# Scores issued sooner and in pairs, transposes behind the units with fixed keys: a two-layer recurrent and attention block on one core

## The chip, the cores and the metric

The kernel runs on one core of one Trainium2 chip. The time is the device time in microseconds of one execution; three runs of the kernel before gave 791.44 to 791.93 us, with a median of 791.5. Most executions of a kernel agree within 0.3%.

## What is computed

The input has 16 sequences of 256 tokens with 256 features. Layer 0 normalises, runs a complex diagonal recurrence with 32 states beside a feed-forward part of 1024 units with GELU, and adds the product of the two. Layer 1, where the change is, does for each sequence:

```
q  = xn @ Wq                       # 16 heads, 128 plain + 64 rotary columns
kv = xn @ Wkv_a                    # 64 latent + 64 rotary columns
c  = rmsnorm(kv[:64]);  k_rope = rope(kv[64:])
scores = causal(q . k) / sqrt(192);  attn = softmax(scores)
s  = (attn @ v) @ Wo
z  = xn @ base_w + base_b + 2 * sum_e gate_e * (xn @ A_e) @ B_e   # top 2 of 8 experts
x  = x + s * silu(z)
```

The weights of keys and values are folded into those of queries and output beforehand, so the scores are taken against the latent (64) and rotary (64) columns, and the weighted sum is one over latents.

## The kernel before

**Steps.** Layer 1 runs in steps n = 10b + m: sequence b, m from 0 to 9. Each engine has its own program (one function for each block), with the same loop over n, and semaphores between them. Every engine runs its instructions in the order written. In step n TensorE issues, in this order (L889 to L923): LoRA's projection `lo` of the next sequence (m = 8); the weighted sum `pv` of the sequence before, in four banks v0 to v3 (m = 5); query blocks `q0` to `q7` of the next sequence (m = 2: q1, q2; 3: q3, q0; 6: q5; 7: q7; 9: q6, q4); unit n of the scores; `tk`, the transposes of the next sequence's keys (m = 8); `ty`, four transposes of the normalised rows of the sequence after next (m = 6); `mi`, the small projections that give latents, rotary keys, LoRA's inner part and the router (m = 8 and 9); `tm`, two transposes of LoRA's gated inner part (m = 6); and `o0`, `o1`, the output blocks of the sequence before (m = 6 and 7). Query, output, LoRA and small projections are made of three FP32R products each (L549).

**Units.** A sequence has ten units of scores: four W (two tiles of 224 and 256 columns' worth of keys, queries as weights), four M (three tiles of 128, 160 and 192), both at L773, and two T, "with fixed keys" (L766), where the keys are the weights, 32 columns of the array for each head, and which are issued together at m = 5. Unit n goes to one of two banks, n modulo 2, and waits for the maximum of unit n - 2 (`mx`, L1610). Then VectorE masks and takes the maximum (L1608), ScalarE the exponential (L1065), VectorE the reciprocal (L1615), GpSimd the product (`normalise`, L2051), VectorE the turn (L1631, L1644), each for its own unit in the order of n. The sums of the weighted sum are split by ScalarE (oh, L1078) and VectorE (ol, L1653) into a high and a low part, pair 0 and pair 1 of banks for the first half of the queries (qt = 0), then for the second (EVAC, L51).

**The ring.** All jobs of TensorE but the scores take turns in six banks of PSUM, in the order of `shared_bank_order` (L142), which is the order of issue. `free_shared` (L659) makes job k wait until job k - 6 has been read. For v0, `freed_by` (L340) asks for `oth` and `otl` up to pair 0 of both halves, the third of four.

**VectorE's step** (L1809 to L1857): subtractions of the latents (m = 5), `y_low` (m = 7), `gated_out`, the turning of queries (L1579), the gate's thread, reciprocal, turn of weights, `weigh` (L1561), `gate_sum` (L1556, m = 8, needs `lo`), and last the maximum of unit n.

**GpSimd's step** (L2146 to L2168): the key's turn (L2022, m = 1), which waits for the two small projections as ScalarE copied them, the factors of the norms (L2083 to L2103, m = 1 and 2), the gate's product (L2038, m = 5), sums of queries (L2044, L2045), residual (L2113), `normalise(n - 2)`.

Of the kernel before, what the change touches and what calls it, by code (L numbers as in the profile page):

```python
# [15 lines left out]
NB = 16  # L16
# [22 lines left out]
UNITS = 10  # L39
# [7 lines left out]
TOTAL = NB * UNITS  # L47
# [8 lines left out]
Q0_AT = {}  # L56
LAST_LORA, LAST_SUM, LAST_SPREAD = 152, 153, 149
KV_AT, GATE_AT, SCALE_AT, NORM_AT, YN_AT = 1, 2, 6, 0, 4
TURN_AT, TM_AT, TK_AT, LORA_AT, MISC_AT = 6, 6, 8, 8, (8, 9)
GATE_REST = 9  # L60
PRODUCT_AT = 5

TURN_FIRST = (5, 13, 20, 28, 36, 44, 52)
BU_AT = (7, 14, 20, 28, 36, 44, 52, 60)
# [72 lines left out]
def with_next(n):  # L137

    return UNITS <= n < TOTAL - 1 and unit(n)[1] == unit(n + 1)[1] == "T"


def shared_bank_order():  # L142

    js = [
        ("q", 1), ("q", 3), ("ty", 1), ("q", 0), ("q", 5), ("q", 7), ("q", 2), ("q", 4), ("lo", 0), ("mi", 2), ("mi", 3), ("q", 6),
    ]
    for n in range(STEPS):
        b, m = n // UNITS, n % UNITS
        if (d := lora_of(n)) is not None:
            js.append(("lo", d))  # L150
        if (d := due("V", n, 0)) is not None:

            if len(js) % 2:
                js.append(("pad", len(js)))
            js += [("v", 4 * d + i) for i in range(4)]
        js += [("q", u) for u in Q0_AT.get(n, ())]
        if b + 1 < NB:
            js += [("q", 8 * (b + 1) + u) for u in queries_at(b + 1, m)]
        if m == TK_AT and b + 1 < NB:
            js.append(("tk", b + 1))  # L160
        if m == TURN_AT and b + 2 < NB:
            js.append(("ty", b + 2))
        if m in MISC_AT and b + 2 < NB:
            js.append(("mi", 2 * (b + 2) + MISC_AT.index(m)))
        if m == TM_AT and b + 1 < NB:
            js.append(("tm", b + 1))
        for qt in range(2):
            if (d := due("O", n, qt)) is not None:
                js.append(("o", 2 * d + qt))
    return js  # L170
# [27 lines left out]
def build(nc, x, consts, rows, vecs, w1t, w2t, b1c, bt, ct, nuth, wqn, wkbt, wqr, wkva, wvbt, wo,  # L198
          baset, lorab, loraa, routert, out):
    ctx = ExitStack()  # L200
    with ctx:
# [134 lines left out]
        def jof(kind, i):  # L336
            return bank[ring[jplace[(kind, i)] % RING]]
# [206 lines left out]
        def _(e):  # L544
# [232 lines left out]
            def l1_pv(b, blocks, units):  # L777

                first, end = blocks
                C = C4[b % 2]  # L780
                w.wait_ge("pt", UNITS * b + units)
                w.wait_ge(f"c{b % 2}", 256 * (b // 2 + 1))
                for i in range(4):
                    free_shared("v", 4 * b + i)
                if blocks == LAST_BLOCKS:

                    w.wait_ge("otl", 4 * b + 2)
                for kb in range(end):
                    q = max(first, kb)
                    at = slice(64 * (kb % 2), 64 * (kb % 2) + 64)  # L790
                    for i in range(4):
                        rows_ = slice(32 * i, 32 * i + 32)
                        sums = jof("v", 4 * b + i).rearrange("p (u t) -> p u t", u=2)
                        for half in range(2):
                            j = e.matmul(sums[64 * half:64 * half + 64, :, 32 * q:32 * end],  # L795
                                         C[rows_, kb // 2, at], PT[rows_, 2 * half:2 * half + 2, kb, q:end, :],
                                         start=(kb == 0), stop=(kb == end - 1), skip_group_check=True)
                j.then_inc(SEM["pv"], 1)
# [19 lines left out]
            for g in range(L0_STEPS):  # L818
# [40 lines left out]
                c, r = divmod(g - 6, 8)  # L859
                if r == 0 and 0 <= c < NC - 1:  # L860
                    l0_turn(c + 1, 1)
                if g in TURN_FIRST and g != 13:
                    c = TURN_FIRST.index(g)
# [25 lines left out]
            for n in range(STEPS):  # L889
                b, m = n // UNITS, n % UNITS  # L890
                if (d := lora_of(n)) is not None:
                    l1_lora(d)
                for qt in range(2):
                    if (d := due("V", n, qt)) is not None and (qt or d == NB - 1):
                        if d < NB - 1:
                            l1_pv(d, ALL_BLOCKS, UNITS)
                        else:
                            l1_pv(d, LAST_BLOCKS if qt else FIRST_BLOCKS, UNITS if qt else FIRST_DONE)
                for u in Q0_AT.get(n, ()):
                    l1_q(0, u)  # L900
                if b + 1 < NB:
                    for u in queries_at(b + 1, m):
                        l1_q(b + 1, u)
                if n < TOTAL and not (n and with_next(n - 1)):
                    l1_s(n)
                    if with_next(n):
                        l1_s(n + 1)
                if m == TK_AT and b + 1 < NB:
                    free_shared("tk", b + 1)
                    l1_tk(b + 1, jof("tk", b + 1))  # L910
                if m == TURN_AT and b + 2 < NB:
                    free_shared("ty", b + 2)
                    l1_turn(b + 2, jof("ty", b + 2))
                if m in MISC_AT and b + 2 < NB:
                    i = 2 * (b + 2) + MISC_AT.index(m)
                    free_shared("mi", i)
                    l1_misc(b + 2, i % 2, jof("mi", i))
                if m == TM_AT and b + 1 < NB:
                    free_shared("tm", b + 1)
                    l1_tm(b + 1, jof("tm", b + 1))  # L920
                for qt in range(2):
                    if (d := due("O", n, qt)) is not None:
                        l1_out(2 * d + qt)  # L923

        @block.scalar
        def _(e):
# [258 lines left out]
            for n in range(STEPS):  # L1185
                b, m = n // UNITS, n % UNITS
                if n == 5:
                    place(e, w, 1, 0, (2, 3))
                c, i = b, m
                if 0 <= c < NB - 1 and i == TM_AT:  # L1190
                    mids(c + 1, jof("tm", c + 1))
                c, i = b, m
                if 0 <= c < NB - 2 and i == TURN_AT:
                    y_high(c + 2, jof("ty", c + 2))
                c, i = divmod(n - 1, UNITS)
                if 0 <= c < NB - 1 and i == TK_AT:
                    keys(c + 1, jof("tk", c + 1))
                for u in Q0_AT.get(n - 1, ()):
                    if u % 2 == 0:
                        queries(0, u)  # L1200
                if n == TOTAL - UNITS:
                    exps(n - 1)
                c, i = divmod(n - 1, UNITS)
                if 0 <= c < NB - 1:
                    for u in queries_at(c + 1, i):
                        if u % 2 == 0:
                            queries(c + 1, u)
                if n and (d := sum_of(n - 1)) is not None:
                    gate_tanh(d)
                if m == YN_AT and b + 2 < NB:  # L1210
                    normed(b + 2)
                for qt in range(2):
                    if (d := due("L", n, qt)) is not None:
                        latents(d, qt)
                if m == SCALE_AT and b + 1 < NB:
                    weighed(b + 1)
                c, i = divmod(n - 1, UNITS)
                if 0 <= c < NB - 2 and i in MISC_AT:
                    t = MISC_AT.index(i)
                    misc(c + 2, t, jof("mi", 2 * (c + 2) + t))  # L1220
                if 0 <= n - 1 < TOTAL and n != TOTAL - UNITS:
                    exps(n - 1)
                c, i = divmod(n - 1, UNITS)
                if 0 <= c < NB - 1 and i == GATE_AT:
                    gate_exp(c + 1)
# [634 lines left out]
        def _(e):  # L1860
# [287 lines left out]
            for n in range(STEPS):  # L2148
                b, m = n // UNITS, n % UNITS
                if m == KV_AT and b + 1 < NB:  # L2150
                    key_turn(b + 1)
                    chain = factors(b + 2)
                go(chain, 3)
                if m == PRODUCT_AT and b + 1 < NB:
                    gate_product(b + 1)
                for u in Q0_AT.get(n - 1, ()):
                    if u % 2 == 1:
                        queries_sum(0, u // 2)
                c, i = divmod(n - 1, UNITS)
                if 0 <= c < NB - 1:  # L2160
                    for u in queries_at(c + 1, i):
                        if u % 2:
                            queries_sum(c + 1, u // 2)
                for qt in range(2):
                    if (d := due("C", n, qt)) is not None:
                        residual(2 * d + qt)
                if 0 <= n - 2 < TOTAL:
                    normalise(n - 2)  # L2168


def shape_constants():
# [86 lines left out]
```

## Time and profile before

| what | value |
|---|---|
| median of 3 runs | 791.5 us |
| profiled execution, its own time | 791.67 us |
| its span, first to last instruction | 789.9 us |
| busy of the span: TensorE, its weight load | 778.6 us, 711.5 us |
| VectorE, ScalarE, GpSimd | 681.7, 524.5, 479.5 us |
| TensorE's granted clock | 0.999 of full speed |
| chain that ended last, share of TensorE | 92% |

The profiled execution lies 1.77 us above its span and 0.17 us above the median. Layer 0 fills the first 260 us or so, layer 1 the rest; steps of layer 1 repeat sequence by sequence. A busy TensorE is one whose matmuls follow each other without a gap, whatever each of them costs.

### The profile page before, as it was taken

How to read it: one execution, taken by the hardware profiler on the slowest of the kernel's cores; microseconds unless marked ns; L12 is line 12 of the kernel's file. 1: busy time of each engine (PE TensorE's matmuls, PEld its weight loads, DVE VectorE, ACT ScalarE, POOL GpSimd, SP SyncE). 2: the span in 40 equal slices, each digit the busy share in tenths (PEclk: the TensorE clock that was granted, in tenths of full speed). 3: DMA queues.
4: the chain of work that ended last, by engine and by line, in shares of the span. 5: the costliest groups of instructions: out<-in, count | busy, mean ns of one | idle time of the engine just before them, and what ended most of it. 6: DMA issues, size and time to landing. Idle time of an engine off the chain costs nothing.

```text
span 789.9 us, 23152 instructions
## 1 busy us (share of the span) xinstructions
PE 778.6 (99%) x7976; PEld 711.5 (90%) x7976; DVE 681.7 (86%) x2616; ACT 524.5 (66%) x1612; POOL 479.5 (61%) x1278
## 2 busy tenths in 40 slices
PE   9999999999999999999999999999999999999988
PEld 7889889888889889898998989899898998989867
DVE  6998897888688899989898998989989898998885
ACT  5554454445555787777767777677777867777682
POOL 6880202202236696776867768686776867768673
PEclk9999999999999999999999999999999999999999
DMA  8600220000002222322222322223222222322220
GB/s 302 253 2 2 62 82 27 1 1 1 1 15 52 40 46 52 61 54 36 48 46 50 64 39 50 40 46 55 56 55 35 48 46 49 63 39 53 34 52 28
DMA packets 101334, 41.15 MB, mean 52 GB/s; under 512 B 91744, under 2 KB 98400, under 8 KB 100576
## 3 DMA queue, kind: packets, MB, share of 16 engines
q1 hardware_dynamic: 98896, 38.89, 22.1%
q8 instruction: 63, 1.03, 0.5%
q10 hardware_dynamic: 2320, 0.79, 0.4%
q14 instruction: 55, 0.45, 0.2%
HBM read 14.47 MB, written 4.19 MB: 24 GB/s over the span
## 4 chain that ended last, share of the span: by engine, by line
PE 92%; DVE 4%; ACT 1%; POOL 1%; issue 1%; ACTq 0%; POOLq 0%; DVEq 0%
PE bank L549 63%; PE bank L773 11%; PE bank L795 8%; PE bank L766 3%; PE bank L629 2%; PE bank L815 1%; PE bank L566 1%; DVE SM L1608 1%; PE bank L681 1%; ACT SM L1065 1%; DVE PT L1631 1%; PE bank L641 1%; PE bank L655 1%; POOL SM L2051 1%; PE bank L700 0%
## 5 line engine op out<-in xcount | busy, mean ns | idle before, releaser
L1065 ACT ACTIVATE SM<-SM,stb 128x224 f32<-128x224 f32 (+7 forms) x512 | 207.2, 407 | 62.7 <-DVE stb L1608 58.2
L2051 POOL TENSOR_SCALAR SM<-SM,stb 128x224 f32<-128x224 f32 (+7 forms) x512 | 195.2, 396 | 67.5 <-DVE stb L1615 66.1
L549 PE MATMUL bank<-yh,wq_lo 128*128 128x256 f32 x512 | 150.6, 294 | 0.0
L549 PE MATMUL bank<-yh,wq_hi 128*128 128x256 f32 x512 | 144.7, 283 | 0.0
L549 PE MATMUL bank<-yl,wq_hi 128*128 128x256 f32 x512 | 144.6, 282 | 0.0
L773 PE MATMUL bank<-KT,QT 128*128 128x192 f32 (+4 forms) x640 | 120.9, 327 | 1.7 <-DVE stb L1608 1.7
L1608 DVE CUSTOM_DVE_ANT_0 SM<-bank,CONST 128x224 f32<-128x224 f32 (+3 forms) x320 | 97.2, 348 | 23.3 <-PE bank L773 20.9
L1631 DVE STREAM_TRANSPOSE PT<-SM 128x128 f32<-128x128 f32 (+2 forms) x232 | 99.7, 462 | 16.7 <-PE bank L795 16.7
L773 PEld LDWEIGHTS bank<-KT,QT 128*128 128x128 f32 x640 | 97.5, 190 | 5.3 <-DVE stb L1608 3.6
L549 PEld LDWEIGHTS bank<-yh,wq_lo 128*128 128x128 f32 x512 | 97.1, 190 | 1.4
L549 PEld LDWEIGHTS bank<-yh,wq_hi 128*128 128x128 f32 x512 | 97.1, 190 | 0.0
L549 PEld LDWEIGHTS bank<-yl,wq_hi 128*128 128x128 f32 x512 | 97.0, 189 | 0.0
L1065 ACT ACTIVATION_READ_ACCUMULATOR SM<-SM,stb 128x1 f32 x512 | 96.9, 189 | 0.0
L950 ACT ACTIVATE hs<-bank,B 128x512 f32<-128x512 f32 x64 | 44.0, 688 | 75.3 <-PE bank L549 70.2
L2044 POOL TENSOR_TENSOR QA<-QA 128x256 f32<-128x256 f32 x62 | 45.9, 740 | 58.7 <-DVE QA L1579 58.7
L1037 ACT ACTIVATE QT<-bank 64x512 f32<-64x512 f32 x128 | 75.6, 590 | 6.5 <-PE bank L549 5.0
L1579 DVE TENSOR_TENSOR QA<-bank,TR 128x512 f32<-128x512 f32 x124 | 79.4, 683 | 0.1
L549 PE MATMUL bank<-woe_hi,ol 128*128 128x256 f32 x256 | 75.4, 294 | 0.7 <-issue 0.7
L549 PE MATMUL bank<-w2h,hl 128*128 128x256 f32 x256 | 74.0, 289 | 0.2 <-DVE w2l L1352 0.2
L549 PE MATMUL bank<-w2h,hh 128*128 128x256 f32 x256 | 72.4, 283 | 0.0
L549 PE MATMUL bank<-w2l,hh 128*128 128x256 f32 x256 | 72.3, 283 | 0.0
L549 PE MATMUL bank<-woe_hi,oh 128*128 128x256 f32 x256 | 72.1, 281 | 0.0
(229 smaller groups left out, 2068.9 us busy)
## 6 DMA issues: line engine op xcount, KB each, us to landing
QT<-QA SPq DMA_DIRECT2D x240, 64.0 KB, 2.1
PT<-KV SPq DMA_DIRECT2D x256, 16.0 KB, 1.8
out<-fo SPq DMA_DIRECT2D x32, 128.0 KB, 2.0
X<-in_x SPq DMA_DIRECT2D x7, 512.0 KB, 11.5
stage<-in_wqn SPq DMA_DIRECT2D x2, 1024.0 KB, 5.3
stage<-in_wo SPq DMA_DIRECT2D x2, 1024.0 KB, 4.9
stage<-in_w1t SPq DMA_DIRECT2D x4, 256.0 KB, 5.0
stage<-in_w2t SPq DMA_DIRECT2D x2, 512.0 KB, 6.2
```

Of the source, the lines that this page charges most:

```text
L549: i = e.matmul(dst, a, b, start=(first and j == 0), stop=(last and j == 2), skip_group_check=skip)
L766: j = e.matmul(sbank[n % 2][32 * i:32 * i + 32, at:to], KT[b % 3][:, p, 32 * kb:32 * kb + 32], Q[:, :, kb:3, i, :], start=True, stop=True)
L773: j = e.matmul(sbank[n % 2][:, at], Q[:, q, :, :].rearrange("p h c -> p (h c)"), KT[b % 3][:, p, 0:32 * q + 32], start=True, stop=True)
L795: j = e.matmul(sums[64 * half:64 * half + 64, :, 32 * q:32 * end], C[rows_, kb // 2, at], PT[rows_, 2 * half:2 * half + 2, kb, q:end, :], ...
L950: e.activation(hs[g % 2][:, :], fbank[g % 2][:, :], ACT.Gelu, bias=B1[:, g % 8:g % 8 + 1]).then_inc(SEM["gelu"], 1)
L1037: i = e.activation(QT[r, (2 * b + g // 2) % 3, p, :, g % 2:4:2, :].rearrange("p n j c -> p j n c"), src[r, :, :, :], ACT.Copy)
L1065: i = e.activation(M[:, at], M[:, at], ACT.Exp, bias=S[:, 0, j:j + 1], scale=-1.0, accum_out=S[:, 1, j:j + 1])
L1579: i = e.tensor_tensor(A[:, part, :, :, g % 2, :], src, TR[:, part, :].rearrange("p (n c) -> p n c", n=8).unsqueeze(1).broadcast_to([128, 2 ...
L1608: i = e.tensor_tensor_reduce(M[:, at], bk[:, at], mask[:, 224 - 32 * q:256], 1.0, 3e38, ALU.add, ALU.min, S[:, 0, j:j + 1])
L1631: return e.transpose(PT[:, slot, 0:k, q:q + some, :].rearrange("p k q c -> p q k c"), src)
L2044: e.tensor_tensor(A[:, 0, 0, :, :], A[:, 0, 0, :, :], A[:, 1, 1, :, :], ALU.subtract)
L2051: i = e.tensor_scalar(P[:, at], P[:, at], S[:, 2, j:j + 1], 1.0, ALU.mult, ALU.mult)
```

## The change

Constants, the helper that says which units a step issues, the order of the ring and the two loops change. The order of the ring and TensorE's program are the same list, written twice.

- Units: for b = 2 to 14 nothing is issued at m = 0, 1 and 2 (b = 14: units 0 and 1 of the last sequence sooner); the step m = 7 issues units 7 and 8, m = 8 unit 9 and the next sequence's unit 0, m = 9 the next one's units 1 and 2.
- `ty` and `tm` go ahead of the step's query block (from b = 1), so they come directly behind the T units of m = 5. At b = 0 `tm` stays last.
- `tk` goes from m = 8 to m = 7 (from b = 1), behind the scores; `mi` goes ahead of the scores (from b = 1).
- GpSimd: `PRODUCT_AT` from 5 to 4, and the call goes from ahead of the sums of queries to behind `normalise`.

```diff
-TURN_AT, TM_AT, TK_AT, LORA_AT, MISC_AT = 6, 6, 8, 8, (8, 9)
+TURN_AT, TM_AT, TK_AT, TK_FIRST, LORA_AT, MISC_AT = 6, 6, 7, 8, 8, (8, 9)
-PRODUCT_AT = 5
+PRODUCT_AT = 4
+def scores_at(n):
+    if not 0 <= n < TOTAL:
+        return ()
+    b, m = divmod(n, UNITS)
+    if b and m < 3 and b > 1 and (b < NB - 1 or m < 2):
+        return ()
+    if b and b < NB - 1 and m > 6:
+        return {7: (n, n + 1), 8: (n + 1, n + 2), 9: (n + 2, n + 3) if b < NB - 2 else (n + 2,)}[m]
+    if n and with_next(n - 1):
+        return ()
+    return (n, n + 1) if with_next(n) else (n,)
+def tk_of(n):
+    b, m = divmod(n, UNITS)
+    return b + 1 if m == (TK_AT if b else TK_FIRST) and b + 1 < NB else None
...
+                if m == TURN_AT and b + 2 < NB:
+                    free_shared("ty", b + 2)
+                    l1_turn(b + 2, jof("ty", b + 2))
+                if m == TM_AT and b and b + 1 < NB:
+                    free_shared("tm", b + 1)
+                    l1_tm(b + 1, jof("tm", b + 1))
                 for u in Q0_AT.get(n, ()):
                     l1_q(0, u)
                 if b + 1 < NB:
                     for u in queries_at(b + 1, m):
                         l1_q(b + 1, u)
-                if n < TOTAL and not (n and with_next(n - 1)):
-                    l1_s(n)
-                    if with_next(n):
-                        l1_s(n + 1)
...
-                if m in MISC_AT and b + 2 < NB:
+                if m in MISC_AT and 0 < b and b + 2 < NB:
                     i = 2 * (b + 2) + MISC_AT.index(m)
                     free_shared("mi", i)
                     l1_misc(b + 2, i % 2, jof("mi", i))
...
+                for i in scores_at(n):
+                    l1_s(i)
+                if tk_of(n):
+                    free_shared("tk", tk_of(n))
+                    l1_tk(tk_of(n), jof("tk", tk_of(n)))
...
-                if m == PRODUCT_AT and b + 1 < NB:
-                    gate_product(b + 1)
...
                 if 0 <= n - 2 < TOTAL:
                     normalise(n - 2)
+                if m == PRODUCT_AT and b + 1 < NB:
+                    gate_product(b + 1)
```

The order of the ring (`shared_bank_order`) changes in the same way.

## Rows read from the trace of the kernel before

**Rows 1.** TensorE's waits, 290 to 750 us: us in total, times, longest

```profile
PE bank L795 <- DVE PT L1631: 0.4, 1, 0.4
```

**Rows 2.** Busy time by engine in one step, from one weighted sum to the next

```profile
core 0: us, PE busy (x) PEld busy (x) DVE busy (x) ACT busy (x) POOL busy (x), PEclk, DMA share, GB/s
494.14:528.08 33.94, 33.94 (x400) 31.75 (x399) 30.49 (x141) 25.26 (x89) 24.93 (x66) 1.00 0.26 49
```

**Rows 3.** Timeline of TensorE behind that weighted sum: start, busy us, line, what, count

```profile
498.29 1.52 PE L766 MATMUL bank<-QT,KT 128*32 128x192 f32 x48
499.74 0.38 PE L549 MATMUL bank<-yh,wq_lo 128*128 128x256 f32 x1
499.96 0.28 PE L549 MATMUL bank<-yl,wq_hi 128*128 128x256 f32 x1
...
501.27 0.60 PE L681 MATMUL bank<-CONST,yn 128*128 128x128 f32 x4
501.71 0.38 PE L706 MATMUL bank<-CONST,ML 128*128 128x128 f32 x2
501.84 0.37 PE L549 MATMUL bank<-woe_hi,ol 128*128 128x256 f32 x1
502.05 0.28 PE L549 MATMUL bank<-woe_lo,oh 128*128 128x256 f32 x1
```

**Rows 4.** Timeline of VectorE in the same stretch; the last row is the third subtraction alone

```profile
498.41 0.71 DVE L1631 STREAM_TRANSPOSE PT<-SM 128x512 f32<-128x512 f32 x1 [1.20 <-PE bank L795]
499.04 2.71 DVE L1653 TENSOR_TENSOR ol<-bank,oh 128x512 fp32r<-128x512 f32 x4
...
500.46 0.69 DVE L1653 TENSOR_TENSOR ol<-bank,oh 128x512 fp32r<-128x512 f32 x1
```

**Rows 5.** Timeline of TensorE at b = 0, transposes directly behind a fixed-key unit

```profile
266.38 0.66 PE L681 MATMUL bank<-CONST,yn 128*128 128x128 f32 x4
```

**Rows 6.** Timelines around a unit that waited for a maximum, b = 1

```profile
280.79 0.08 DVE L1608 DVE_READ_ACCUMULATOR2_ANT stb<- 128x1 f32 x1
...
280.92 0.19 PEld L773 LDWEIGHTS bank<-KT,QT 128*128 128x128 f32 x1 [0.78 <-DVE stb L1608]
...
280.93 0.49 PE L773 MATMUL bank<-KT,QT 128*128 128x128 f32 x2 [0.38 <-DVE stb L1608]
```

**Rows 7.** Timeline of TensorE: units 8, 0 and 1, 2, 7

```profile
478.08 0.97 PE L773 MATMUL bank<-KT,QT 128*128 128x224 f32 x4
478.89 0.38 PE L700 MATMUL bank<-CONST,KV 128*128 128x128 f32 x2
...
484.22 1.79 PE L773 MATMUL bank<-KT,QT 128*128 128x224 f32 x10
...
485.97 0.28 PE L549 MATMUL bank<-yl,wq_hi 128*128 128x256 f32 x1
...
488.73 0.98 PE L773 MATMUL bank<-KT,QT 128*128 128x128 f32 x6
...
489.67 0.28 PE L549 MATMUL bank<-yl,wq_hi 128*128 128x256 f32 x1
...
506.21 0.98 PE L773 MATMUL bank<-KT,QT 128*128 128x128 f32 x6
```

**Rows 8.** Timeline of VectorE: the gate's sum, unit 8's maximum; unit 6's maximum

```profile
478.28 0.69 DVE L1556 TENSOR_TENSOR PT<-bank,VEC 128x512 f32<-128x512 f32 x1
479.09 0.39 DVE L1608 CUSTOM_DVE_ANT_0 SM<-bank,CONST 128x224 f32<-128x224 f32 x1
...
479.75 0.08 DVE L1608 DVE_READ_ACCUMULATOR2_ANT stb<- 128x1 f32 x1
...
506.67 0.08 DVE L1608 DVE_READ_ACCUMULATOR2_ANT stb<- 128x1 f32 x1
```

**Rows 9.** Timeline of GpSimd: the key's turn and the gate's product

```profile
485.50 0.45 POOL L2022 TENSOR_TENSOR kr<-ML,rope_c 128x128 f32<-128x128 f32 x1
...
499.27 0.61 POOL L2038 TENSOR_TENSOR ML<-ML,lg 128x256 f32<-128x256 f32 x1
```

**Rows 10.** Timeline of VectorE at b = 14, maximum of unit 9

```profile
751.75 0.39 DVE L1608 CUSTOM_DVE_ANT_0 SM<-bank,CONST 128x224 f32<-128x224 f32 x1 [0.70 <-PE bank L773]
```

More of the change, by code:

```diff
@@ L155, in shared_bank_order @@
             js += [("v", 4 * d + i) for i in range(4)]
+        if m == TURN_AT and b + 2 < NB:
+            js.append(("ty", b + 2))
+        if m == TM_AT and b and b + 1 < NB:
+            js.append(("tm", b + 1))
         js += [("q", u) for u in Q0_AT.get(n, ())]
@@ L158, in shared_bank_order @@
             js += [("q", 8 * (b + 1) + u) for u in queries_at(b + 1, m)]
[L159 to L162, printed above, removed]
+        if tk_of(n):
+            js.append(("tk", tk_of(n)))
         if m in MISC_AT and b + 2 < NB:
             js.append(("mi", 2 * (b + 2) + MISC_AT.index(m)))
-        if m == TM_AT and b + 1 < NB:
-            js.append(("tm", b + 1))
+        if n == TM_AT:
+            js.append(("tm", 1))
         for qt in range(2):
@@ L898, in _ @@
                             l1_pv(d, LAST_BLOCKS if qt else FIRST_BLOCKS, UNITS if qt else FIRST_DONE)
+                if m == TURN_AT and b + 2 < NB:
+                    free_shared("ty", b + 2)
+                    l1_turn(b + 2, jof("ty", b + 2))
+                if m == TM_AT and b and b + 1 < NB:
+                    free_shared("tm", b + 1)
+                    l1_tm(b + 1, jof("tm", b + 1))
                 for u in Q0_AT.get(n, ()):
@@ L903, in _ @@
                         l1_q(b + 1, u)
-                if n < TOTAL and not (n and with_next(n - 1)):
-                    l1_s(n)
-                    if with_next(n):
-                        l1_s(n + 1)
[L908 to L913, printed above, removed]
-                if m in MISC_AT and b + 2 < NB:
+                if m in MISC_AT and 0 < b and b + 2 < NB:
                     i = 2 * (b + 2) + MISC_AT.index(m)
@@ L917, in _ @@
                     l1_misc(b + 2, i % 2, jof("mi", i))
-                if m == TM_AT and b + 1 < NB:
-                    free_shared("tm", b + 1)
-                    l1_tm(b + 1, jof("tm", b + 1))
+                for i in scores_at(n):
+                    l1_s(i)
+                if tk_of(n):
+                    free_shared("tk", tk_of(n))
+                    l1_tk(tk_of(n), jof("tk", tk_of(n)))
+                if n in MISC_AT:
+                    i = 4 + MISC_AT.index(m)
+                    free_shared("mi", i)
+                    l1_misc(2, i % 2, jof("mi", i))
+                if n == TM_AT:
+                    free_shared("tm", 1)
+                    l1_tm(1, jof("tm", 1))
                 for qt in range(2):
@@ L1194, in _ @@
                     y_high(c + 2, jof("ty", c + 2))
-                c, i = divmod(n - 1, UNITS)
-                if 0 <= c < NB - 1 and i == TK_AT:
-                    keys(c + 1, jof("tk", c + 1))
+                if n and tk_of(n - 1):
+                    keys(tk_of(n - 1), jof("tk", tk_of(n - 1)))
                 for u in Q0_AT.get(n - 1, ()):
```

## The prediction

> **What bounds the kernel now.** I read the waits of TensorE first, then its own rows over one step of the second layer, then the engines that feed it. Between 290 and 750 us, thirteen and a half steps of one sequence each, TensorE waited once, 0.4 us [rows 1]. From one weighted sum (L795) to the next it takes 33.94 us and is busy for 33.94 [rows 2]; the clock is at the upper level (2.4 GHz) throughout. The stream itself is the bound there: a reordering can gain only what the stream loses where one kind of matmul follows another, and any wait that it makes is paid in full. VectorE is busy for 30.49 of the 33.94 us, so it can't catch up much. Last I read the order in which PSUM banks go round: job k of the shared list waits for job k-6.
>
> **The change, part by part**, for the steps n = 10b + m with b = 1 to 13, which are 13 steps alike.
>
> *The ring of six banks.* Both orders have 20 jobs a step, 4 of them the weighted sums v0 to v3. Behind them came q5, ty, tm, o0, q7, o1; so tm took over v0's bank. Now it is ty, tm, q5, o0, q7, tk: ty and tm take banks of q3 and q0, long read, and q5 takes v0's. freed_by gives v0's bank free after the third of the four subtractions of L1653, since pair 0 is read for both halves of the queries. VectorE waits 1.20 us for the end of the weighted sum, turns one unit's weights (0.71) and subtracts from 499.04 on; the third ends at 500.46 + 0.69 = 501.15 [rows 4]. Before, tm started at 501.71, behind it. Now to q5: the fixed-key units run 498.29 to 499.74, the four transposes ty take 0.44 and 0.06 for the exit (below), tm 0.13, and the second matmul of q5 would come 0.21 later (as 501.84 to 502.05): 499.74 + 0.50 + 0.13 + 0.21 = 500.58 [rows 3]. With the wait: a released weight load starts 0.05 us after the write that it waits for (280.79 + 0.08 to 280.92), and a restarted pair of matmuls takes 0.49 us [rows 6] against 0.38 for one in the stream [rows 7], so 0.10 are lost besides. A query matmul takes 0.12 in the stream ((501.27 - 499.96)/11). So the second matmul starts at 501.15 + 0.05 + 0.10 + 0.12 = 501.42, late by 0.84 us. Bounds: with no restart 0.74; with the whole load of 0.19 [rows 6] in place of the 0.10, 0.93. Queued behind q5 on TensorE are the output block o0, q7 and all scores, none of which can pass. 13 x 0.84 = 10.9 us (9.6 to 12.1). In b = 14 there is no ty, q7 gets that bank 1.4 us later, and nothing waits.
>
> *Exit of the fixed-key units.* Before, q5 came behind them: its first matmul was 0.22 from the next, not 0.12, so 0.10 lost [rows 3]. At b = 0 the transposes already stood there: four took 0.66 us [rows 5] against 0.60 [rows 3], 0.06 lost. Gain 0.04 to 0.05 a step, -0.6 us in all (0 to -1.3, if nothing or all of it goes).
> The Trainium skill, TensorEngine Tiling (Array Packing), Key Properties, says that changing the tiling mode drains the TensorE. The trace shows that something is paid in both orders; by the rule what follows makes no difference, the -0.6 would be 0 and the forecast 803.7.
>
> *Pairs of scores.* Unit W plus M in a row took 484.22 to 485.97 with the first query matmul, 1.75. M alone took 488.73 to 489.67, 0.94, and W alone 478.08 to 478.89, 0.81: together 1.75 too [rows 7]. So joining costs and gains 0.00; the resolution of the rows leaves +-0.01 per join, two joins a step, +-0.3 us. I take 0.
>
> *What the early units wait for.* Each unit needs the maximum (L1608) of the one two before it, since two banks are used in turn. In step m = 8 VectorE runs the gate's sum (L1556) ahead of the maximum of unit 8, and that sum needs LoRA's end, which now comes behind units 7 and 8 (before, unit 8 was behind it too, but unit 0 of the next sequence far later). Let L be LoRA's end. The sum starts at L + 0.20 (478.08 to 478.28) and takes 0.69; the maximum, 479.09 to 479.83, takes 0.74 and could follow with an overlap of 0.08 (479.09 was a wait for unit 8 itself): ready at L + 1.55 [rows 7, 8]. TensorE comes to unit 0 after six matmuls of the small projections (0.74) and unit 9 (0.81): L + 1.55. Load at L + 1.60 and the restart's 0.10 make it 0.15 late: 13 x 0.15 = 2.0 us (0 to 3.3, if VectorE is 0.1 later). Units 1 and 2 have q6, q4 and the second projection, 3.6 us, ahead of them; I take 0, up to the same 0.15 each. Unit 8, now directly behind unit 7, would start 0.82 after 506.21, at 507.03, and needs the maximum of unit 6, which ends at 506.75 [rows 7, 8]; the shift by 0.84 makes that safe.
>
> *The gate's product on GpSimd.* PRODUCT_AT goes from 5 to 4, but the call also goes from ahead of step 5's unit to behind step 4's. In both orders it stands between normalise(2) and normalise(3), with nothing else between them (the chain of factors is done at m = 2). That part does nothing. What moves the product is the transfer of the score units: GpSimd's thread from the key's turn to the product's end takes 485.50 to 499.88, 14.38 us [rows 9]. It starts 1.28 us after the second small projection ends (484.22), and from there to the next weighted sum it was 9.92 us (494.14, [rows 2]); one unit less in between leaves 9.11. So the product ends 1.28 + 14.38 - 9.11 = 6.55 us after the weighted sum's start (before 5.74), and tm, which now comes at 6.10 (4.15 + 1.45 + 0.50), waits 0.5. This hides behind q5's bank, which is free at 501.20 - 494.14 = 7.06, by about 0.1 us; without the bank's wait it costs 0.5 a step, 6 us. I count 0 here.
>
> *Transposes of the keys a step sooner, projections ahead of the scores.* tk behind unit 8 needs v3's bank (free by 501.75 [rows 4]) and the keys scaled on ScalarE, long done. Its copies to KT are ready before unit 0 wants them. DMAs stay: SP's issues hang on the queries' turns and the scaled latents, and none of these changes its step. Price 0.
>
> *The end.* From b = 14 on TensorE waits for VectorE. There VectorE idled 0.70 us for unit 9's scores [rows 10], which are now issued ahead of q4: -0.7 us (0 to -1.2). First sequence: only q5 and ty swap, 0.
>
> **Sum.** 10.9 + 2.0 - 0.6 - 0.7 = +11.6 us on the profiled execution's 791.67, which makes 803.3; the median of the runs is 0.17 lower, so 803.1 us, 1.5% slower.
>
> **The rivals.**
> 1. *GpSimd later still.* Its thread is in series and has a margin of 0.1 us at tm. If the second projection's copy or the factors come 0.5 us later, the product ends at 7.05, the second matmul of q5 at 7.05 + 0.05 + 0.10 + 0.24 + 0.21 = 7.65 in place of 7.28: +0.4 a step, 5 us: 808. For it: the thread is one chain on one engine, with nothing to leave out. Against: its start hangs on ScalarE, which now has the copies of the keys behind it sooner.
> 2. *The other side: the bank is free in time, and the order pays.* Place: q5 behind tm. Needed: the third subtraction ended by about 500.3, 2.0 us after the weighted sum (it decides at that point). Then the wait is gone; if the product comes too, what stays is -0.6, -0.7 and, if a join saves 0.06 us of the change of kind, 13 x 2 x 0.06 = -1.6: 788.6. For it: TensorE's stream is all that bounds these steps. Against: a turn of 0.71 and three subtractions of 0.69 stand in series on VectorE behind the sum, more than 2.0, and the joins showed 0.00.
> 3. *Nothing moves.* As 2, with no gain from joins, or a small wait that eats it: 791.7 - 1.3 = 790.4, up to 793.
> 4. *Only the product's wait.* The bank is free but GpSimd late: 0.5 x 13 - 1.3 = +5: 796.8. Against: as 2.
>
> **Numbers.** Forecast 0.72, rival 1 0.13, rival 4 0.05, rival 3 0.04, rival 2 0.06. The forecast's own bounds (9.6 + 0 - 1.3 - 1.2 = +7.1 to 12.1 + 3.3 + 2 x 13 x 0.15 = +19) give 799 to 811 at their ends, which don't fall together; with rival 1 inside, 8 in 10 lie in 797.5 to 809.5. Within 0.2% (1.6 us, about what a measurement tells from no change) of 791.5: 0.04, faster 0.06, slower 0.90.
>
> **What would show it.** On the changed trace: a wait of TensorE's load at L549 (q5) for VectorE's L1653, 13 times, 0.5 to 0.9 us each with a period of 34.8 to 35.0 us from one weighted sum to the next; the four transposes behind the fixed-key units at 0.66; a small wait at L773 for L1608 in the middle of each step; GpSimd's product ending 6.3 to 6.6 us after the weighted sum's start. If q5 starts without a wait, the bank's step is wrong and with it the sign; if tm (L706) is the longer wait, rival 1 holds.

## The result, and the profile after

The changed kernel took 804.83 us (median of 5 runs, 804.76 to 805.07) against 791.44 of the kernel before beside it (791.34 to 791.93): a ratio of 1.0164, 95% interval 1.0153 to 1.0175, so 13.4 us slower. 803.1 us was forecast. Every ratio below is against executions of the kernel before in the same session (medians 791.62 to 791.85 us); one of the 11 executions of run 8 took 1970.57 us and is left out of its ratio.

| | before | after |
|---|---|---|
| span | 789.9 | 803.3 |
| 13 steps, first to fourteenth weighted sum | 440.94 (33.92 each) | 454.80 (34.98 each) |
| from there to the fifteenth (b = 14) | 26.86 | 26.37 |
| the rest | 31.46 | 31.42 |

The span's 13.4 us are 13.86 in the 13 steps, less 0.49 in b = 14; nothing else moved. The clock is 1.00 in both.

Busy time by engine of the changed kernel, once over one step (to be compared with [rows 2]) and once over the 13 steps; below them those 13 of the kernel before. Columns: stretch and length, then busy us of each engine.

```profile
core 0: us, PE busy (x) PEld busy (x) DVE busy (x) ACT busy (x) POOL busy (x), PEclk, DMA share, GB/s
500.53:535.52 34.99, 34.50 (x399) 31.59 (x398) 29.78 (x141) 25.09 (x90) 24.90 (x66) 1.00 0.25 47
...
290.66:745.46 454.80, 448.26 (x5175) 410.72 (x5175) 385.47 (x1779) 327.64 (x1159) 324.77 (x846) 1.00 0.26 48
```

```profile
290.64:731.58 440.94, 440.94 (x5174) 412.48 (x5174) 394.35 (x1779) 329.50 (x1159) 325.08 (x847) 1.00 0.26 49
```

TensorE, which was busy without a gap, now isn't; its matmuls are the same in number (to one). The idle time shown (6.5 us) is under half of what the steps lost (13.9), since a matmul whose successor waits is drawn as busy until its own end. So the price of a wait must be read from the distance between starts. TensorE's waits of the changed kernel, 290 to 760 us, in place of [rows 1]:

```profile
PE bank L730 <- POOL ML L2066: 3.5, 13, 0.6
PE bank L573 <- DVE ol L1681: 3.0, 12, 0.3
PE bank L819 <- DVE PT L1659: 0.5, 1, 0.5
```

Two are new: the transposes tm (now L730) for the gate's product on GpSimd, and the query block (L573) for the subtraction (now L1681). Timeline of TensorE behind the weighted sum that starts at 500.53, in place of [rows 3]:

```profile
504.68 1.52 PE L790 MATMUL bank<-QT,KT 128*32 128x192 f32 x48
506.13 0.66 PE L705 MATMUL bank<-CONST,yn 128*128 128x128 f32 x4
507.00 0.41 PE L730 MATMUL bank<-CONST,ML 128*128 128x128 f32 x2 [0.21 <-POOL ML L2066]
507.69 0.36 PE L573 MATMUL bank<-yh,wq_lo 128*128 128x256 f32 x1 [0.28 <-DVE ol L1681]
507.88 0.28 PE L573 MATMUL bank<-yl,wq_hi 128*128 128x256 f32 x1
```

VectorE in that stretch, in place of [rows 4]; the last row is again the third subtraction alone:

```profile
504.80 0.71 DVE L1659 STREAM_TRANSPOSE PT<-SM 128x512 f32<-128x512 f32 x1 [1.34 <-PE bank L819]
505.43 2.70 DVE L1681 TENSOR_TENSOR ol<-bank,oh 128x512 fp32r<-128x512 f32 x4
...
506.85 0.69 DVE L1681 TENSOR_TENSOR ol<-bank,oh 128x512 fp32r<-128x512 f32 x1
```

The third subtraction ends at 507.54, 7.01 us after the weighted sum's start, as before to the hundredth. q5's first load starts behind it (PEld is TensorE's weight load):

```profile
507.65 0.19 PEld L573 LDWEIGHTS bank<-yh,wq_lo 128*128 128x128 f32 x1 [0.49 <-ACT oh L1107]
```

The view names ScalarE here, the engine of another of its semaphores; the copies had ended, and the subtraction ends 0.11 before the load. q5's second matmul stands at 7.35 us after the sum's start; 7.28 was forecast, and 6.44 without the wait (both worked out, not measured).

GpSimd's thread, the key's turn and the gate's product (now L2050 and L2066), in place of [rows 9]:

```profile
492.58 0.56 POOL L2050 TENSOR_TENSOR kr<-ML,rope_c 128x128 f32<-128x128 f32 x1 [2.08 <-ACT ML L1044]
...
506.20 0.65 POOL L2066 TENSOR_TENSOR ML<-ML,lg 128x256 f32<-128x256 f32 x1
```

It takes 14.27 us (14.38 before), now after a wait of 2.08 for the small projection's copy, and the product ends at 6.32 after the sum's start (5.74 before, 6.55 forecast). tm waits for it, but q5 would have waited longer anyway. The first of the 13 steps is the exception that the list hides: there the product ends at 6.74 us, tm waits 0.63, and q5 then has no wait of its own in the list, though its load again starts 0.11 to 0.12 us after the third subtraction's end. The two waits end together there.

The other place is unit 0 behind unit 9. VectorE's gate's sum (now L1584) and the maximum of unit 8, in place of [rows 8]:

```profile
520.49 0.69 DVE L1584 TENSOR_TENSOR PT<-bank,VEC 128x512 f32<-128x512 f32 x1 [1.89 <-PE bank L573]
521.10 0.38 DVE L1636 CUSTOM_DVE_ANT_0 SM<-bank,CONST 128x224 f32<-128x224 f32 x1
...
521.75 0.08 DVE L1636 DVE_READ_ACCUMULATOR2_ANT stb<- 128x1 f32 x1
```

VectorE stood still for 1.89 us ahead of the sum, waiting for LoRA, while unit 8's scores lay ready. Units 9 and 0 on TensorE then, in place of [rows 7], and the first weight load of unit 0:

```profile
521.02 2.00 PE L797 MATMUL bank<-KT,QT 128*128 128x224 f32 x8
522.67 0.47 PE L573 MATMUL bank<-yh,wq_lo 128*128 128x256 f32 x1
```

```profile
521.94 0.19 PEld L797 LDWEIGHTS bank<-KT,QT 128*128 128x128 f32 x1 [0.35 <-issue]
```

The maximum ends at 521.83 and the load starts 0.11 to 0.12 us later. The view names no releaser here, and the list of TensorE's waits has no row for this wait.

### The profile page after: what moved, and what is told of

Same layout as the page of the kernel before. It is cut to its first block, busy times and chain, and to the rows that moved or that the text cites. A ratio compares the mean times of both kernels' runs of the same rounds, so it can differ in the third digit from the quotient of the medians.

```text
span 803.3 us, 23167 instructions
## 1 busy us (share of the span) xinstructions
PE 784.7 (98%) x7976; PEld 709.0 (88%) x7976; DVE 672.5 (84%) x2616; ACT 522.2 (65%) x1612; POOL 480.4 (60%) x1278
## 4 chain that ended last, share of the span: by engine, by line
PE 85%; DVE 6%; POOL 3%; ACT 3%; issue 2%; DMA 0%; ACTq 0%; POOLq 0%; DVEq 0%
PE bank L573 62%; PE bank L797 12%; PE bank L819 7%; DVE ol L1681 2%; PE bank L653 2%; DVE PT L1659 1%; POOL SM L2079 1%; ACT oh L1107 1%; ACT SM L1094 1%; PE bank L590 1%; DVE SM L1636 1%; PE bank L665 1%; PE bank L679 1%; POOL QA L2072 0%; POOL QA L2073 0%
## 5 line engine op out<-in xcount | busy, mean ns | idle before, releaser
L573 PE MATMUL bank<-yh,wq_lo 128*128 128x256 f32 x512 | 150.6, 294 | 3.0 <-DVE ol L1681 3.0
L573 PE MATMUL bank<-yh,wq_hi 128*128 128x256 f32 x512 | 144.3, 282 | 0.0
L573 PE MATMUL bank<-yl,wq_hi 128*128 128x256 f32 x512 | 144.2, 282 | 0.0
L797 PE MATMUL bank<-KT,QT 128*128 128x192 f32 (+4 forms) x640 | 119.1, 329 | 1.8 <-DVE stb L1636 1.8
L573 PEld LDWEIGHTS bank<-yh,wq_lo 128*128 128x128 f32 x512 | 96.8, 189 | 5.8 <-ACT oh L1107 5.5
L573 PEld LDWEIGHTS bank<-yl,wq_hi 128*128 128x128 f32 x512 | 96.9, 189 | 0.3
L573 PEld LDWEIGHTS bank<-yh,wq_hi 128*128 128x128 f32 x512 | 96.8, 189 | 0.0
L573 PE MATMUL bank<-w2h,hl 128*128 128x256 f32 x256 | 74.0, 289 | 0.2 <-DVE w2l L1380 0.2
L573 PE MATMUL bank<-woe_hi,ol 128*128 128x256 f32 x256 | 73.4, 287 | 0.7 <-issue 0.7
L573 PE MATMUL bank<-w2h,hh 128*128 128x256 f32 x256 | 72.4, 283 | 0.0
L573 PE MATMUL bank<-w2l,hh 128*128 128x256 f32 x256 | 72.3, 283 | 0.0
L573 PE MATMUL bank<-woe_hi,oh 128*128 128x256 f32 x256 | 72.1, 281 | 0.0
```

The lines of the kernel that those rows point to most:

```text
L573: i = e.matmul(dst, a, b, start=(first and j == 0), stop=(last and j == 2), skip_group_check=skip)
L797: j = e.matmul(sbank[n % 2][:, at], Q[:, q, :, :].rearrange("p h c -> p (h c)"), KT[b % 3][:, p, 0:32 * q + 32], start=True, stop=True)
```

## The experiments

The edits are shown shortened, one line for each job; `...` marks what is left out.

**1. The old order of turns and query block, early scores kept (q5_first).** Against the changed kernel, in `shared_bank_order` and in TensorE's program:

```diff
-    ty(b + 2); tm(b + 1); queries_at(b + 1, m)
+    queries_at(b + 1, m); ty(b + 2); tm(b + 1)
```

> The changed kernel with the order q5, ty, tm of before, in TensorE's program and in the ring; scores early and in pairs as changed. Bank theory (the wait of q5 for v0's bank is the loss): tm takes v0's bank again, read 0.5 us before it comes; what stays is unit 0's wait of 0.14 us a step, so 34.06 us from one weighted sum to the next and 792.3 us. Rival, early scores are the loss (VectorE and GpSimd can't follow): 34.8 or more and about 803. Rival, the product is the loss: tm comes 1.4 us later than in the changed kernel, so it can't wait either, and this run doesn't tell it from the bank.

Measured: 802.31 us, ratio 1.0132 (1.0118 to 1.0146), 34.78 us a step. By the number that is the rival's forecast (34.8 or more, about 803), but this run doesn't show its cause: q5 and tm wait for nothing, and the loss has a place that none of the theories named. TensorE's only repeated wait in the list, then its rows and VectorE's in one step:

```profile
PE bank L573 <- DVE QA L1607: 4.9, 13, 0.4
```

```profile
512.83 0.38 PE L724 MATMUL bank<-CONST,KV 128*128 128x128 f32 x2
513.58 0.39 PE L573 MATMUL bank<-woe_hi,ol 128*128 128x256 f32 x1 [0.37 <-DVE QA L1607]
```

```profile
511.64 0.69 DVE L1519 TENSOR_TENSOR yl<-bank,yh 128x512 fp32r<-128x512 f32 x1
512.25 1.28 DVE L1607 TENSOR_TENSOR QA<-bank,TR 128x512 f32<-128x512 f32 x2
```

The block behind tk is o1. tk, moved ahead of it, has taken v3's bank, which was o1's; six jobs back from o1 is now q5, and q5 is turned on VectorE until 513.53, where TensorE was ready at 512.97. In the changed kernel six back from o1 is ty, read 1.2 us sooner (512.33 here). So this run moved the wait to another pair of jobs, and my expectation had looked at three jobs of the ring and not at all twenty. It leaves the rival (the early scores) open; runs 5 and 6 test it.

**2. The turns ahead of q5 and nothing else (turns_alone).** Against the kernel before:

```diff
+    ty(b + 2); tm(b + 1)      # tm from b = 1; ty at b = 0 too
     queries_at(b + 1, m)
     ... scores, tk ...
-    ty(b + 2)
     ... mi ...
-    tm(b + 1)
```

At b = 0 ty is ahead of q5 as well, here and in the changed kernel; only tm stays last there.

> The kernel before with ty and tm ahead of q5 alone; scores, keys' transposes, projections and product where they were. Bank theory: q5 waits for the third subtraction, 0.84 less 0.05 for the exit: 34.72 us a step, 13 steps, 801.8 us. Product theory (tm waits for the gate's product and q5 behind it): the product ends 5.74 us after the weighted sum's start, ahead of tm at 6.10, so nothing waits and the time is 790.8. Early-scores theory: 791.

Measured: 802.88 us, ratio 1.0140 (1.0126 to 1.0154), 34.81 a step (+0.90). Waits, and TensorE behind a weighted sum that starts at 499.26; GpSimd's product in the last fence:

```profile
PE bank L551 <- DVE ol L1658: 8.4, 12, 0.9
PE bank L708 <- POOL ML L2043: 0.6, 1, 0.6
```

```profile
504.86 0.66 PE L683 MATMUL bank<-CONST,yn 128*128 128x128 f32 x4
505.35 0.38 PE L708 MATMUL bank<-CONST,ML 128*128 128x128 f32 x2
506.41 0.36 PE L551 MATMUL bank<-yh,wq_lo 128*128 128x256 f32 x1 [0.68 <-DVE ol L1658]
506.61 0.28 PE L551 MATMUL bank<-yl,wq_hi 128*128 128x256 f32 x1
```

```profile
504.36 0.64 POOL L2043 TENSOR_TENSOR ML<-ML,lg 128x256 f32<-128x256 f32 x1
```

Here the product ends at 505.00, 5.74 after the sum, and tm runs without a wait at 505.35; q5's second matmul still stands at 7.35, to the hundredth where it is in the changed kernel. So the bank of v0 is enough to make the wait, and the product's wait in the changed kernel is inside it. The row with 0.6 us for the product is the first of the 13 steps, where the product ends at 6.74 us in this kernel too; no other step has one. One later step took 35.00 us and not 34.8 (its wait is the 0.9 of the list); why is open. The early scores are not needed for 11.0 of the 13.4 us (11.6 in the 13 steps).

**3. The product's call where it was (product_back).** Against the changed kernel:

```diff
-PRODUCT_AT = 4
+PRODUCT_AT = 5
...
                 go(chain, 3)
+                if m == PRODUCT_AT and b + 1 < NB:
+                    gate_product(b + 1)
...
                     normalise(n - 2)
-                if m == PRODUCT_AT and b + 1 < NB:
-                    gate_product(b + 1)
```

> The changed kernel with the gate's product where it was in GpSimd's program (ahead of step 5's sums). By my reading the two places are the same order of instructions: 804.8, the changed kernel's time, within 0.2. If the place counts: the product later by one normalise (1.2 us), tm later by 1.2, some 12 us more: 817.

Measured: 805.06 us, ratio 1.0165 (1.0150 to 1.0181); 13 steps in 454.76 us against 454.80. The ratio is that of the changed kernel (1.0164), and the 817 us of the other reading are far off. "A step sooner" is the same place in GpSimd's order.

**4. ty alone ahead of q5 (ty_alone).** Against the kernel before: ty goes ahead of `queries_at`, tm stays behind, ring alike.

> The kernel before with ty alone ahead of q5 (ty, q5, tm), also in the ring: tm keeps v0's bank. Only the exit of the fixed-key units changes: 0.04 to 0.05 us a step less, 33.88 a step, 790.8 us. Rival, the drain is paid alike whatever follows: 791.4.

Measured: 791.04 us, 11 runs, ratio 0.9991 (0.9982 to 1.0000); 13 steps in 440.54 us against 440.94, so 0.03 a step less, 0.4 us in all. It has the right sign and is a little less than expected (0.04 to 0.05); the total's interval touches 1, and the distances between weighted sums (33.87 to 33.90, before 33.90 to 33.93) carry the reading. What follows the fixed-key units does matter here, by 0.03 us a step.

**5. q5_first with tk behind o1 (q5_first_tk_last).** To see whether the wait found in 1 was the whole of it:

```diff
-    tk(b + 1)                 # behind the scores of m = 7
     o0 / o1
+    tk(b + 1)                 # from b = 1
```

> The run q5_first (order q5, ty, tm) took 34.8 us a step and not 34.06: its output block o1 waits for the turning of q5, since tk, moved ahead of o1, hands o1 the bank of q5 (TensorE at L573 waits for VectorE's L1607, 13 times). Here tk goes behind o1, in the program and in the ring, all else as in q5_first. Bank theory: both ring waits gone, unit 0's 0.14 us stays: 34.06 a step, 792.5 us. Rival, early scores are a loss whatever the ring: 34.7 or more, 801 to 802.

Measured: 796.48 us, ratio 1.0058 (1.0044 to 1.0072). The 13 steps took 443.52 us, 34.12 each, without a repeated wait; that is the bank theory's 34.06 and not its rival's 34.7. The total missed mainly because b = 14 took 29.19 us and not 26.4. There the last sequence's keys come too late. ScalarE, which copies them ahead of its next exponentials, stands 3.21 us for tk (0.35 in run 6); VectorE then stands 3.28 us for an exponential; and on TensorE one unit of M kind waits 0.44 us for the copy of the keys and the next one 1.50 for a maximum:

```profile
751.97 0.38 ACT L1060 ACTIVATE KT<-bank 128x256 f32<-128x256 f32 x1 [3.21 <-PE bank L726]
```

```profile
755.76 0.18 DVE L1648 RECIPROCAL stb<-stb 128x3 f32<-128x3 f32 x1 [3.28 <-ACT SM L1099]
```

```profile
753.19 1.09 PE L799 MATMUL bank<-KT,QT 128*128 128x128 f32 x6 [0.44 <-ACT KT L1062]
...
757.21 1.09 PE L799 MATMUL bank<-KT,QT 128*128 128x128 f32 x6 [1.50 <-DVE stb L1641]
```

So tk's place ahead of o1 serves the end, which I had not weighed.

**6. The changed kernel with ty, q5, tm (ty_only_ahead).** One swap: tm behind the query block instead of ahead.

> The changed kernel with one swap: ty, q5, tm in place of ty, tm, q5, in program and ring. q5 then takes q0's bank, tm takes v0's 0.5 us after it is read, and o1 takes ty's, read at 13.2 us where o1 comes at 13.7. Bank theory: no ring wait at all; unit 0's 0.14 a step stays, the exit gains 0.04: 34.02 a step, 791.8 us. Early-scores theory: 801 to 802.

Measured: 793.15 us, 11 runs, ratio 1.0016 (1.0008 to 1.0025), 34.08 a step. One swap of two transposes gives back 11.7 of the 13.4 us with all scores issued as in the change. Its only repeated wait left is unit 0's, and that costs 0.22, not 0.14 (run 7); this makes 1.0 of the 1.35 us by which the time is over what was expected. With runs 5 and 6 the early scores, as a loss whatever the ring, are ruled out.

**7. As 6, the gate's sum behind the maximum (ty_ahead_sum_last).**

```diff
+                if n < TOTAL:
+                    most(n)
                 if (d := sum_of(n)) is not None:
                     gate_sum(d)
-                if n < TOTAL:
-                    most(n)
```

> As ty_only_ahead, and on VectorE the gate's sum (L1584) behind the maximum of the step's unit in place of ahead of it. If unit 0 waits because the maximum of unit 8 stands behind the sum, which waits for LoRA, that wait goes: 33.88 a step, and with b = 14 and the end 1.0 us shorter than before as in the changed kernel, 790.0 us. Rival, the sum comes too late for ScalarE's tanh and for weigh (L1589), and unit 1 waits instead: 34.0 or more, 791.5 to 793.

Measured: 790.98 us, 11 runs, ratio 0.9991 (0.9982 to 1.0000), 33.86 a step: 0.22 less than in 6. Units 9 and 0 in this run, against the 2.00 us and 1.65 from start to start in the changed kernel:

```profile
513.29 1.78 PE L797 MATMUL bank<-KT,QT 128*128 128x224 f32 x8
514.72 0.47 PE L573 MATMUL bank<-yh,wq_lo 128*128 128x256 f32 x1
```

So the gate's sum ahead of the maximum is unit 0's whole wait. But the stretch between the last two full weighted sums rose from 14.50 to 15.09 us, so the time is 1.0 us over the 790.0 expected.

**8. The same, but for the last sequence (sum_last_but_end).** In the last sequence's step the sum is ahead of the maximum again.

> As ty_ahead_sum_last (33.85 us a step, but 15.09 in place of 14.50 us between the last but one and the last full weighted sums), with the gate's sum ahead of the maximum again in the last sequence's step alone. If that one placement made the end longer, it comes back to 14.50 and the time to 790.4 us, under both kernels; if the end is longer for another reason, 791.0.

Measured: 790.23 us, ratio 0.9979 (0.9970 to 0.9989), 1.5 us under the kernel before; that stretch is 14.49 again. TensorE is busy throughout the steps, as at the start:

```profile
core 0: us, PE busy (x) PEld busy (x) DVE busy (x) ACT busy (x) POOL busy (x), PEclk, DMA share, GB/s
290.49:730.57 440.08, 440.08 (x5174) 411.66 (x5174) 394.71 (x1779) 326.21 (x1159) 326.15 (x848) 1.00 0.26 49
```

This is the version that beats both kernels: 0.86 us less in the 13 steps, 0.4 in b = 14.

## Why the prediction was right

The sign, the place and the size came from two readings: TensorE had no idle time to pay a wait with, and the order of the ring gave q5 a bank whose reader's end could be read off. By its terms:

| step of the prediction | forecast | measured |
|---|---|---|
| q5 waits for v0's bank | 13 x 0.84 = 10.9 | 7.35 - 6.44 (worked out) = 0.91 a step, 11.8; run 2, exit included: 452.57 - 440.94 = 11.6 |
| exit of the fixed-key units | -0.6 | -0.4 (run 4) |
| joins of units | 0 (+-0.3) | not measured alone; run 8 (440.08) is 0.5 under run 4 (440.54), with every other move in it |
| unit 0 behind the gate's sum | 13 x 0.15 = 2.0 | 13 x 0.22 = 2.9 (run 7 against 6) |
| the product's place | 0 | 0 (run 3) |
| tm's wait for the product | 0, hidden | 0, hidden: the same 7.35 with it and without (run 2) |
| the end | -0.7 | -0.49, all of it in b = 14 |
| sum | +11.6 | 11.6 + 2.9 - 0.5 - 0.5 = +13.5; span +13.4 |

The first -0.5 of that sum is the remainder of run 8, whose cause is open. At b = 14 VectorE's 0.70 us ahead of unit 9 are gone, but just before it VectorE now stands 0.39 us for ScalarE; that this is why the end gave 0.49 and not 0.7 is not shown.

**What was off, and why.** Both waits were too small by 0.07 us each. I took 0.05 us from the write to the load that it releases, from a load that waited for one semaphore [rows 6]. q5's first load started 0.11 after the subtraction's end (507.54 to 507.65). Unit 0's load started 0.11 to 0.12 after the maximum's end (521.83 to 521.94), and the difference is there too: 0.15 forecast, 0.22 measured. Both loads wait for more than one semaphore, and in the trace the last one of them is waited for by a separate semaphore instruction of 0.05 us ahead of the load; the load of [rows 6] waits for its last one itself. From 260 us on, the changed kernel has 39 released loads of the first kind, all 0.11 to 0.12 us after the write, and 9 of the second, all at 0.05. So 0.06 of each 0.07 is this latency. No run took one condition away alone.

**The signs set beforehand.** The period came (34.93 to 35.02 us), the product's end (6.32), and the 0.66 us of the transposes. By the list of waits the sign of rival 1 came too: tm has 3.5 us there, q5 3.0. That sign was badly chosen, since the list gives q5 only what is left once tm has waited. q5's load stood still for 0.49 us and starts 0.11 after the subtraction that frees the bank, and in run 2, where tm doesn't wait, q5 stands at the same place. Rival 1 needed a product that ends at 7.05 us.

**tm.** The product ended 0.2 us sooner than worked out, half of it since the thread took 0.11 less, the rest since it started sooner behind the projection than the 1.28 us of before. The rival "only the product's wait" had its second half come true: had q5's bank been free, tm's wait would have been the price. Its price by itself was not measured, because every kernel run here with tm ahead of q5 has the bank's wait too. An estimate: tm's first matmul starts 0.87 us after ty's in the changed kernel and 0.49 in run 2, so 0.38 a step, about 5 us in 13 steps.

**The Trainium skill's rule** (TensorEngine Tiling (Array Packing), Key Properties: changing the tiling mode drains the TensorE) agrees with a loss at the exit in both orders (0.10 and 0.06 us in [rows 3] and [rows 5]). Read as in the prediction, what follows would make no difference; run 4 shows 0.03 us a step less with the transposes behind, so there the measurement decides. It is small beside the 1.07 us that the step lost.

**The faster rival** needed the third subtraction by 2.0 us after the sum's end. It ended 2.86 after it in both kernels: one turn and three subtractions in a row on VectorE, which start from the weighted sum itself. The new order of the scores did not move it.

**Where the expectations failed.** Run 1 showed that I had followed the ring only around the jobs that the diff had swapped. Each of the twenty jobs gets another neighbour six back when two are swapped or one is moved; ty and tm together make a wait of 0.9 us a step, and tk with the old order of q5 makes one of 0.66 (34.78 of run 1 less 34.12 of run 5). In the changed kernel tk does no harm only because ty, not q5, stands six jobs ahead of o1.

## What to carry to other kernels

Where banks go round in a fixed order, write the table of every job with the job one round back and the end of that one's reader, before and after; a move that is free on its own engine can cost a wait at a job that it never touched. Behind a producer whose result is read slowly, put first as many jobs as banks are free (two here), and make the second a long one: ty, q5, tm had no wait for a bank where ty, tm, q5 lost 0.9 us a step. And an engine that stands still for one input while another lies ready (VectorE's 1.89 us ahead of the gate's sum) can be a sign that two of its instructions are in the wrong order once a neighbour has been moved; swapping them gave 0.22 us a step here, and cost 0.6 at the end until the last sequence was left out.

## What the runs showed of the hardware

- A weight load released by VectorE or GpSimd started 0.05 us after the write where it waited for the last semaphore itself (9 loads of the changed kernel, and [rows 6]), and 0.11 to 0.12 where a separate semaphore instruction ahead of it did (39 loads).
- Four transposes directly behind column-tiled matmuls took 0.63 to 0.66 us against 0.60 in the stream, in every kernel that had them there.
- A short wait can lie wholly inside what the profile draws as busy: unit 0's wait lengthened eight matmuls from 1.78 (run 7) to 2.00 us of busy time, and the list of waits has none of it.
